# A routing stage in another order: two buffers, the division three trips ahead, the output projection first

## The reference

```python
out = jnp.einsum('bhst,bthd->bshd', attn, v)      # 16 heads of 16, divided by the softmax's sum
X = X + ctx @ wo                                  # output projection and residual
h2 = rmsnorm(X, norm2_w).reshape(B * S, d)        # x * rsqrt(mean(x * x) + 1e-6) * w
logits = h2 @ router_w                            # 8 logits a token
...
return X + moe_out                                # and the tower adds h + ffn(layernorm(h))
```

## Time and profile before

| | us |
|---|---|
| median of 3 runs | 795.88 |
| lowest and highest | 795.6, 796.54 |
| profiled execution, its own time | 796.95 |
| its span, first to last instruction | 795.1 |
| TensorE busy in the span | 747.8 (94%) |
| VectorE, ScalarE, GpSimd busy | 464.6, 372.8, 187.8 |

### The profile page before, as it was taken

The page is one execution under the profiler, slowest core; times in us unless marked ns, Lnnn a source line. Parts: engine busy times, 40 slices in busy tenths (PEclk is TensorE's granted clock), DMA queues, the critical chain, the costliest instruction groups (busy, mean ns, idle before and its releaser), DMA issues. The chain is left out here.

```text
span 795.1 us, 19240 instructions
## 1 busy us (share of the span) xinstructions
PE 747.8 (94%) x7245; PEld 563.5 (71%) x7246; DVE 464.6 (58%) x1113; ACT 372.8 (47%) x616; POOL 187.8 (24%) x292
## 2 busy tenths in 40 slices
PE   3899999999999998999998989999999999999994
PEld 1377777777767886455545754555799999999993
DVE  7777777767636555999964874711344444444441
ACT  4677777777633443476773323210333333333330
POOL 5400000000003443333320230165222323223232
PEclk8599999999999999999999999999999999999998
DMA  5400000000011346444466900022523233232331
GB/s 166 171 2 2 2 3 2 3 2 2 3 48 41 107 133 173 124 127 123 121 229 205 318 0 17 13 88 80 167 40 53 47 46 53 40 53 47 46 47 20
DMA packets 70545, 58.97 MB, mean 74 GB/s; under 512 B 7553, under 2 KB 62153, under 8 KB 70481
## 3 DMA queue, kind: packets, MB, share of 16 engines
q1 hardware_dynamic: 62048, 47.61, 19.6%
q0 software_dynamic: 7152, 9.38, 7.2%
q10 hardware_dynamic: 1280, 1.08, 0.4%
HBM read 35.02 MB, written 22.95 MB: 73 GB/s over the span
## 5 line engine op out<-in xcount | busy, mean ns | idle before, releaser
L1474 POOL DMA_INDIRECT out<-ex_Y,ex_to x39 | 60.6, 1553 | 166.1 <-DVE ex_Y L1749 163.0
L652 ACT ACTIVATE la_PT<-ps 128x512 f32<-128x512 f32 x128 | 69.5, 594 | 46.5 <-PE ps L553 46.1
L1214 DVE TENSOR_REDUCE fa_m<-ps 128x2 bf16<-128x512 f32 x128 | 84.2, 682 | 6.7 <-PE ps L1083 5.5
L1703 DVE TENSOR_TENSOR ex_hT<-ps,ex_sl 128x512 f32<-128x512 f32 x39 | 27.0, 691 | 99.0 <-PE ps L1540 99.0
L1184 ACT ACTIVATE fa_PT<-ps 128x1024 f32<-128x1024 f32 x64 | 65.5, 1024 | 39.5 <-PE ps L1098 39.0
L1547 PE MATMUL ps<-WD,ex_hT 128*128 x312 | 74.0, 380 | 1.6 <-DVE ex_Y L1749 0.8
L1540 PEld LDWEIGHTS ps<-ex_xT,V 128*128 128x128 f32 x640 | 74.5, 192 | 1.2 <-ACT ex_xT L1593 0.2
L1540 PE MATMUL ps<-ex_xT,V 128*128 128x128 f32 x640 | 74.8, 275 | 0.0
L1540 PEld LDWEIGHTS ps<-ex_xT,XS 128*128 128x128 f32 x608 | 70.8, 192 | 0.9
L1540 PE MATMUL ps<-ex_xT,XS 128*128 128x128 f32 x608 | 71.0, 275 | 0.0
L671 DVE TENSOR_TENSOR la_SM<-ps,la_SA 128x512 bf16<-128x512 f32 x64 | 44.3, 692 | 38.1 <-ACT la_SA L634 19.5
(11 more groups left out here) (263 smaller groups left out, 1438.3 us busy)
## 6 DMA issues: line engine op xcount, KB each, us to landing
QK<-qk_parts SPq DMA_DIRECT2D x192, 64.0 KB, 2.3
qk_parts<-pj_parts SPq DMA_DIRECT2D x16, 384.0 KB, 2.8
expert_in<-zfill SPq DMA_DIRECT2D x1, 5070.0 KB, 16.1
ex_XR<-expert_in SPq DMA_DIRECT2D x39, 130.0 KB, 2.0
WG<-in_e_gate SPq DMA_DIRECT2D x8, 512.0 KB, 6.9
WU<-in_e_up SPq DMA_DIRECT2D x8, 512.0 KB, 10.7
WD<-in_e_down SPq DMA_DIRECT2D x8, 512.0 KB, 9.9
out<-HS SPq DMA_DIRECT2D x4, 512.0 KB, 5.5
```

The source lines that it names most:

```text
L652: nc.scalar.activation(PT[:, n // 2 % 2, jh, n % 2], ps[:, 2 * (n % 2) + jh], ACT.Exp, scale=QK_SCALE).then_inc(s_exp[jh], 1)
L1214: nc.vector.reduce_max(m[:, b % 2, grp, 2 * k:2 * k + 2], ps[:, h % 2].rearrange("p (f j) -> p f j", f=2), AX.X).then_inc(s_max, 1)
L1474: nc.gpsimd.indirect_dma_start(out=outs, out_offset=bass.IndirectOffsetOnAxis(ap=to[:, n:n + 1], axis=0), in_=Y[:, n], in_offset=None, com ...
```

## The change

`rt_AT` and `rt_X2` get two buffers each, used by turns. The addition to `HS` moves from VectorE to GpSimd, where it stands ahead of the power and signals `s_res`; the X2 two tiles later waits for that. `rt_hT` goes: ScalarE copies bank 4 straight to `H2T`, and logits reads it there. The increments of `s_apart` go. A trip on TensorE is now output(t+1), logits(t-1), rows(t+3), AT(t+2), normed(t), with identity products in the first and the last trip alone; on VectorE moments(t+1), the division of t+3, hn(t+1), the logits' copy of t; on ScalarE the copy of AT(t+2) ahead of that of normed(t). The loops of VectorE, ScalarE and GpSimd are unrolled.

```diff
-def head_buffers(g, c, nc, tag):
+def head_buffers(g, c, nc, tag, n=1):
...
-    s.AT, s.ATT, s.rec = sb("AT", [P, GT, D]), sb("ATT", [P, DC, GC]), sb("rec", [P, GT * H])
+    s.AT, s.ATT, s.rec = sb("AT", [P, GT, D] if n == 1 else [P, n, GT, D]), sb("ATT", [P, DC, GC]), sb("rec", [P, GT * H])
...
-    (s_in, s_h, s_x2, s_var, s_r2, s_hn, s_ht, s_htc, s_h2, s_lg, s_lgk, s_dv, s_half, s_kept, s_apart) = (
-        sem("rt_" + n) for n in "in h x2 var r2 hn ht htc h2 logits lkept dve half kept apart".split())
+    (s_in, s_h, s_x2, s_var, s_r2, s_hn, s_ht, s_htc, s_lg, s_lgk, s_dv, s_half, s_kept, s_res) = (
+        sem("rt_" + n) for n in "in h x2 var r2 hn ht htc logits lkept dve half kept residual".split())
...
-        s = head_buffers(g, c, nc, "rt_")
+        s = head_buffers(g, c, nc, "rt_", 2)
         st, mv, half = sb("st", [P, GT, 6], F32), sb("mv", [P, GT, 6], F32), sb("half", [P, GT], F32)
-        X2, hn, hT = sb("X2", [P, GT, D], F32), sb("hn", [P, GT, D], F32), sb("hT", [P, DC, GC], F32)
+        X2 = sb("X2", [P, 2, GT, D], F32)
+        hn = sb("hn", [P, GT, D], F32)
...
-                with pool.Fori(0, GN) as t:
+                for t in range(GN):
+                    at = slice(t * GT, (t + 1) * GT)
+                    pool.wait_ge(s_x2, t + 1)
+                    nc.gpsimd.tensor_tensor(g.HS[:, at], g.HS[:, at], X2[:, t % 2], ALU.add).then_inc(s_res, 1)
                     pool.wait_ge(s_var, t + 1)
                     nc.gpsimd.tensor_tensor(mv[:, :, 4], mv[:, :, 3], half[:], ALU.pow).then_inc(s_r2, 1)
-
                     pool.wait_ge(s_hn, t * GT + GT)
-                    nc.gpsimd.tensor_copy(g.XS[:, bass.ds(t * GT, GT), 0:D], hn[:]).then_inc(s_kept, 1)
+                    nc.gpsimd.tensor_copy(g.XS[:, at, 0:D], hn[:]).then_inc(s_kept, 1)
...
+
+                def turn_att(i):
+                    pe.wait_ge(s.at, i + 1)
+                    if i:
+                        pe.wait_ge(s.attc, i)
+                    for k in range(GT):
+                        for c in range(DC):
+                            last = nc.tensor.transpose(ps[:, 2, c * GC + k * P:c * GC + (k + 1) * P], s.AT[:, i % 2, k, c * P:(c + 1) * P], g.identF[:])
+                    last.then_inc(s.att, 1)
...
-                            last = mm(ps[:, 5, k * E:(k + 1) * E], hT[:, cc, k * P:(k + 1) * P], rw[:, cc], start=cc == 0, stop=cc == DC - 1)
+                            last = mm(ps[:, 5, k * E:(k + 1) * E], g.H2T[:, cc, i * GC + k * P:i * GC + (k + 1) * P], rw[:, cc], start=cc == 0, stop=cc == DC - 1)
...
-                for i in range(2):
-                    pe_turn_rows(nc, pe, g, s, i)
-                    if i == 1:
-                        spin(nc, g, 7, 3)
-                        pe.wait_ge(s_in, 48)
-                        output(0)
-                    else:
+                pe_turn_rows(nc, pe, g, s, 0)
+                pe_turn_rows(nc, pe, g, s, 1)
+                spin(nc, g, 7, 5)
+                turn_att(0)
+                spin(nc, g, 7, 2)
+                pe_turn_rows(nc, pe, g, s, 2)
+                spin(nc, g, 7, 2)
+                pe.wait_ge(s_in, 48)
+                output(0)
+                turn_att(1)
+                for t in range(GN):
+                    if t + 1 < GN:
+                        output(t + 1)
+                    if t:
+                        logits(t - 1)
+                    if t + 3 < GN:
+                        pe_turn_rows(nc, pe, g, s, t + 3)
+                    if t + 2 < GN:
+                        turn_att(t + 2)
+                    if t == 0:
+                        spin(nc, g, 7, 4)
+                    elif t == GN - 1:
                         spin(nc, g, 7, 5)
-                    pe_turn_att(nc, pe, g, s, i)
-
-                def trip(t, ahead):
-                    if ahead:
-                        pe_turn_rows(nc, pe, g, s, t + 2)
-                    output(t + 1)
-                    spin(nc, g, 7, 3 if t else 8)
                     turn_normed(t)
-                    if ahead:
-                        pe_turn_att(nc, pe, g, s, t + 2)
-                    logits(t)
-
-                for t in range(GN - 2):
-                    trip(t, True)
-                trip(GN - 2, False)
-                spin(nc, g, 7, 8)
-                turn_normed(GN - 1)
                 spin(nc, g, 7, 3)
                 logits(GN - 1)
                 spin(nc, g, 7, 3)
...
-                    nc.scalar.activation(hT[:], ps[:, 4].rearrange("p (c t) -> p c t", c=DC), ACT.Copy).then_inc(s_htc, 1)
-                    act.wait_ge(s_htc, i + 1)
-                    nc.scalar.activation(g.H2T[:, :, bass.ds(i * GC, GC)], hT[:], ACT.Copy).then_inc(s_h2, 1)
-                    act.wait_ge(s_h2, i + 1)
-
-                for i in range(2):
-                    act_keep_att(nc, act, g, s, i, s_h)
-                with act.Fori(0, GN - 2) as t:
+                    nc.scalar.activation(g.H2T[:, :, i * GC:(i + 1) * GC], ps[:, 4].rearrange("p (c t) -> p c t", c=DC), ACT.Copy).then_inc(s_htc, 1)
+
+                act_keep_att(nc, act, g, s, 0, s_h)
+                act_keep_att(nc, act, g, s, 1, s_h)
+                for t in range(GN):
+                    if t + 2 < GN:
+                        act_keep_att(nc, act, g, s, t + 2, s_h)
                     turned(t)
-                    act_keep_att(nc, act, g, s, t + 2, s_h)
-                for i in range(GN - 2, GN):
-                    turned(i)
...
-                    V.tensor_tensor(X2[:], ps[:, 3].rearrange("p (k d) -> p k d", d=D), g.XS[:, bass.ds(i * GT, GT), 0:D], ALU.add).then_inc(s_x2, 1)
+                    if i >= 2:
+                        dve.wait_ge(s_res, i - 1)
+                    V.tensor_tensor(X2[:, i % 2], ps[:, 3].rearrange("p (k d) -> p k d", d=D), g.XS[:, bass.ds(i * GT, GT), 0:D], ALU.add).then_inc(s_x2, 1)
                     dve.wait_ge(s_x2, i + 1)
                     for k in range(GT):
-                        do(V.bn_stats(st[:, k], X2[:, k]), s_apart)
+                        do(V.bn_stats(st[:, k], X2[:, i % 2, k]))
                         do(V.bn_aggr(mv[:, k, 0:2], st[:, k]))
...
-                    do(V.tensor_tensor(g.HS[:, bass.ds(i * GT, GT)], g.HS[:, bass.ds(i * GT, GT)], X2[:], ALU.add))
...
-                        V.scalar_tensor_tensor(hn[:, k], X2[:, k], mv[:, k, 4:5], w2[:], ALU.mult, ALU.mult).then_inc(s_hn, 1)
+                        V.scalar_tensor_tensor(hn[:, k], X2[:, i % 2, k], mv[:, k, 4:5], w2[:], ALU.mult, ALU.mult).then_inc(s_hn, 1)
...
+                def divide(i):
+                    dve.wait_ge(s.rows, i + 1)
+                    if i:
+                        dve.wait_ge(s.at, i)
+                    rows = ps[:, 0:GT].rearrange("p k (h d) -> p (k h) d", d=PADV)
+                    V.reciprocal(s.rec[:], rows[:, :, DK]).then_inc(s.recip, 1)
+                    dve.wait_ge(s.recip, i + 1)
+                    if i >= 2:
+                        dve.wait_ge(s.att, i - 1)
+                    V.tensor_tensor(s.AT[:, i % 2].rearrange("p k (h d) -> p (k h) d", d=DK), rows[:, :, 0:DK],
+                                    s.rec[:].unsqueeze(2).to_broadcast([P, GT * H, DK]), ALU.mult).then_inc(s.at, 1)
+
                 V.memset(g.LG[0:1, 0, 0:1], 0.0).then_inc(s_lgk, 1)
                 dve.wait_ge(s_lgk, 1)
                 for i in range(2):
-                    dve_divide_heads(nc, dve, g, s, i)
+                    divide(i)
                 moments(0)
+                divide(2)
                 dve.wait_ge(s_in, 48)
                 rms_norm(0)
-
-                def trip(t, ahead):
-                    if ahead:
-                        dve_divide_heads(nc, dve, g, s, t + 2)
-                    moments(t + 1)
-                    rms_norm(t + 1)
+                for t in range(GN):
+                    if t + 1 < GN:
+                        moments(t + 1)
+                    if t + 3 < GN:
+                        divide(t + 3)
+                    if t + 1 < GN:
+                        rms_norm(t + 1)
                     keep_logits(t)
-
-                with dve.Fori(0, GN - 3) as t:
-                    do.enter(t, 3 + 2 * GT)
-                    trip(t, True)
-                do.leave(GN - 3)
-                trip(GN - 3, True)
-                trip(GN - 2, False)
-                keep_logits(GN - 1)
```

## The result

The changed kernel takes 791.3 us in the median of 19 executions, from 788.95 to 795.43, against 795.88 (794.85 to 797.61) before. The ratio is 0.9949, with a 95% interval from 0.9938 to 0.9961: 4.1 us faster (the two medians lie 4.6 apart). That puts it at 791.8, on the upper edge of the predicted range, where 789.5 was forecast: faster by about two thirds of the 6.4 that were forecast. The second thing to see stands beside the median: the executions of the changed kernel spread over 6.5 us, those of the kernel before over 2.8.

What follows compares the result with a forecast made beforehand. VectorE's order was taken to bound the route stage, passing to the TensorE-ScalarE loop. Entry -1.7, trips +7.8, end +0.4 gave 6.4 us saved: 796.95 to 790.5, less 1.07 for the median, 789.5; range 787.8 to 791.8.

Steps and rivals of the forecast that it cites:

- The bound before, and the tail end of the program: VectorE's order sets the route stage's 6.0 us trip; what follows the stage has no slack, so its end moves one for one.
- The entry: Start of the route stage up to the first `hn`: gets longer, 436.2 against 434.48, a loss of 1.7 us.
- The trips: Seven trips between first and last `hn`: five at 4.86 us, two at VectorE's 4.5, 33.3 in all, gaining 7.8.
- The power, the increment, the addition: Power 0.70 to 0.78 us instead of 1.12; dropped increments save 0.2 a trip; the addition on GpSimd costs nothing.
- The rival in which VectorE stays the bound: Power stays 1.12 and the gap behind statistics stays: 5.1 us a trip, 791.4 to 792.6 us; chance 0.14.
- the third: Rival: no wait for ScalarE's copy, all trips at 4.5 us, 787 to 788.5 us; chance 0.12.
- the fifth: Rival: nothing gained, the queued logits' copy holds both cycles near 6 us, 794.3 to 797.5 us; chance 0.04.
- The end: Last `hn` to the stage's last product: 3.9 us against 4.58, plus 0.3 for a 1.2 GHz stretch; gain 0.4.
- The rival of the clock: Clock falls to 1.2 GHz in mid-stage: trips of 9.3 us, 807 us if low from trip 2 on; chance 0.04.
- the 1.07 that the prediction took off for the median: The earlier kernel's median lay 1.07 us below its profiled execution, so the forecast went from 790.5 to 789.5.

Runs made afterwards that it cites:

- AT ahead of rows: The kernel with the filled tail, with AT(t+2) placed ahead of rows(t+3) on TensorE in each trip: 788.47 us median, ratio 0.9908.
- unchanged kernel: The changed kernel itself, run again without any edit as base for the variants: 790.59 us median over six executions, 791.3 over 19.
- filled tail: The changed kernel with identity products added in TensorE's waits of the last two trips: 789.16 us median, ratio 0.9917.
- bare tail: The changed kernel without the identity products of the last trip: 794.09 us median over nine executions, ratio 0.9974.

## Why the prediction was off

By its own steps:

- **The bound before, and the tail end of the program.** Right. The experts' stage took 314.7 us both times.
- **The entry.** 1.7 lost was forecast. The first `hn` came 11.97 us behind the first rows, before 10.39: 1.6 lost.
- **The trips.** VectorE's cycle of 4.5 and TensorE's of 4.86 were forecast; 4.52 (AT ahead of rows) and 4.83 were measured. 41.08 - 33.3 = 7.8 was forecast, 41.08 - 32.88 = 8.2 came, since two of the five middle trips took 4.66 and 4.74. The wait for ATT (0.3 forecast, 0.25) and the output that runs longer behind it are what the loop through ScalarE is made of.
- **The power, the increment, the addition.** 0.70, 0.03 of gap, and hidden: each as taken. The rival in which VectorE stays the bound is out. So are the third, since the output waits for ScalarE, and the fifth, since the logits' copy waits the 0.30 that was reckoned and not over 1 us more.
- **The end.** This step failed. The forecast had 3.9 and, for a stretch at 1.2 GHz, "worth between 0 and 1.7; I take 0.3". At full clock the end took 472.28 - 468.28 = 4.0, as reckoned. But the clock's term was mis-sized. Its average is the distance between the unchanged kernel and the one with a filled tail, 791.3 - 789.16 = 2.1 us with the 19 executions and 790.59 - 789.16 = 1.4 with the six of the same set, in place of 0.3; single executions lost up to 6 (795.43 against 789.15). The low stretch can run on through the last trip into the experts' products: with the bare tail it covered most of 469 to 480, and four such products cost 1.8 and 1.3 more than at full clock. The prediction let it end in the stage, as in the kernel before, and had "behind it the same time as before to the end".
- **The rival of the clock** had the right mechanism and the wrong place. I asked whether the clock would fall in the middle trips, where identity products were taken out, and found them fuller than before. They are, and the granted clock is 1.00 in all of them in every trace taken. The products that mattered are those of the trips that run out of work.

With the filled tail, in whose profile the clock doesn't fall, the time is 789.16: the sum without its failed term was 789.2. That they agree so closely is luck in part: the stage of the profiles saved 7.2 us, where the other parts of the sum had 6.7, and the 1.07 that the prediction took off for the median had no counterpart: the profile of the filled tail, 788.89, lies under its median, not over it.

What stays open: why one execution falls and another of the same program, in which TensorE is busy to the hundredth alike, doesn't; and where in the program the executions at 793 to 795 of the unchanged kernel fell. None of them was profiled. Their mean clock says that they fell, and by as much as the bare tail, whose profile has 0.988 with 11 us at 0.53 and 794.09 us; the place is told by what the filled and the bare tail do. That the filled tail removes them is shown as far as 32 executions go, that the bare tail makes them the rule by nine of nine; the entry's fall was seen once, by chance, and its share was not measured.

## What to carry to other kernels

A change to the order of a stage is priced trip by trip, but its identity products are priced where TensorE runs out of work: the last trips and the seam to the next stage, where a fall of the clock is paid by the next stage's products. Judge such a change by the spread of many executions and not by one profile, which may fall on a short one; fill each wait there, since the products inside a wait cost nothing here (49.14 us with and without). And look at what runs on VectorE beside a small operation of GpSimd that others wait for: here an addition with two SBUF inputs made it half as long again.

## What the runs showed of the hardware

- GpSimd's power over 2 numbers a partition took 0.70 us in 8 of 8 places of the changed kernel, without a VectorE addition of two SBUF operands beside it. With one it took 1.06 to 1.12 in the eight places of the kernel before, and 1.06 in seven and 0.99 in one where the addition was put back. The addition took 0.68 to 0.69 there; no run has it without the power beside it.
- A separate semaphore increment between two dependent VectorE instructions costs 0.11 to 0.12 us (gaps of 0.14 to 0.15 in fifteen of sixteen places, 0.03 in sixteen without it).
- Two executions of one program, with TensorE busy 2.73 us in one window of both and 3.23 and 3.22 in the next, differed in the granted clock: 0.90 and 1.00 in the second.
- GpSimd's float32 addition over 128x512 takes 1.27 us, against 1.16 of its subtraction to bfloat16.
- The stage began between 422.86 and 425.04 us after the start in the traces taken, in code that is the same in all of them: a difference of 2 us in two spans is not yet a gain of the stage.
